# A graph network on one core: ScalarE waits for TensorE's finished products before each half group, and inserts pauses

## The reference, cut to what matters

```python
# layer 0, x is (12500, 128)
msg = relu((x[src] * w[:, None]) @ W_msg + b_msg)
agg = segment_sum(msg, dst, num_segments=12500)
x = layernorm(x + relu(agg @ W_out + b_out))
# layers 1 and 2, with residual and layernorm around both
xt  = einsum('nd,rde->rne', h, W)            # 8 relations
agg = segment_sum(xt[rel, src], dst, num_segments=12500)
h = relu(agg + h @ SW + b)
# out = layernorm(x + h)
```

## Time and profile before

| | us |
|---|---|
| median of 3 runs | 7146.97 (7138.85 to 7151.41) |
| the profiled execution | 7199.0 |
| its span | 7197.2 |
| GpSimdE busy in it | 4549.9 |
| VectorE busy | 2687.2 |
| TensorE matmuls busy | 2514.6 |
| ScalarE busy | 608.2 |

### The profile page before, as it was taken

How to read it: one execution, slowest core, us unless ns; L and a number is a source line. 1 busy time by engine, 2 the same in 40 slices (tenths; PEclk the granted TensorE clock), 3 DMA queues, 4 the chain that set the end, 5 groups by cost and what they waited for, 6 DMA issues and landing times.

```text
span 7197.2 us, 44937 instructions
## 1 busy us (share of the span) xinstructions
PE 2514.6 (35%) x11886; PEld 2050.0 (28%) x11886; DVE 2687.2 (37%) x5889; ACT 608.2 (8%) x1334; POOL 4549.9 (63%) x4832
## 2 busy tenths in 40 slices
PE   4333344333444333433333343333222222222223
PEld 4332233222333322322222233222222222222222
DVE  3777566666555532332222332232111111111112
ACT  2111111111111110000000000000000000000000
POOL 4666666666666646666666666665666666666665
PEclk9666666666666666666666666665556565555556
DMA  5122222222222212222222222221111111121111
GB/s 144 43 79 74 69 73 71 74 70 75 72 72 74 74 58 63 69 69 69 66 70 68 69 69 66 67 68 56 52 51 51 52 51 52 52 53 52 51 51 48
DMA packets 265650, 468.76 MB, mean 65 GB/s; under 512 B 102413, under 2 KB 155317, under 8 KB 265381
## 3 DMA queue, kind: packets, MB, share of 16 engines
q0 software_dynamic: 154016, 315.73, 16.9%
q1 hardware_dynamic: 110212, 149.64, 6.1%
q10 hardware_dynamic: 1152, 0.39, 0.0%
HBM read 343.36 MB, written 122.05 MB: 65 GB/s over the span
## 4 chain that ended last, share of the span: by engine, by line
another core or an unknown queue 48%; DVE 23%; issue 17%; PE 9%; DVEq 2%; ACT 1%; DMA 0%; POOL 0%; SPq 0%; ACTq 0%; POOLq 0%
PE bank L787 5%; DVE rows L763 5%; DVE onehot L745 4%; PE bank L1047 3%; DVE picked L1087 3%; DVE place L1099 2%; DVE tab L1108 1%; DVEq L771 1%; DVE agg L776 1%; DVE bank L1410 1%; DVE work L1411 1%; DVE bank L1408 1%; DVE y L1143 1%; DVE stats L1147 1%
## 5 line engine op out<-in xcount | busy, mean ns | idle before, releaser
L698 POOL DMA_INDIRECT rows<-rel_table,rel_index x3152 | 2973.6, 943 | 1664.4 <-issue 931.5
L787 PE MATMUL bank<-onehot,rows 128*128 128x128 f32 x9626 | 1772.3, 357 | 3320.3 <-issue 1405.4
L787 PEld LDWEIGHTS bank<-onehot,rows 128*128 128x128 f32 x9626 | 1659.1, 265 | 3512.7 <-issue 1537.6
L698 POOL DMA_INDIRECT rows<-msg_table,msg_index x1597 | 1508.8, 945 | 929.0 <-issue 464.7
L776 DVE TENSOR_TENSOR agg<-agg,bank 128x128 f32 x602 | 171.4, 285 | 3613.6 <-remote 3150.7
L745 DVE TENSOR_TENSOR onehot<-bank,place 128x1024 f32<-128x1024 f32 x602 | 728.4, 1210 | 10.6 <-ACT agg L964 3.8
L1047 PE MATMUL bank<-wr,feat 128*128 128x512 f32 x784 | 521.3, 801 | 395.4 <-ACT feat L979 322.0
L763 DVE SCALAR_TENSOR_TENSOR rows<-rows,weight,bank 128x128 f32<-128x128 f32 x1597 | 428.6, 341 | 0.1
L1099 DVE TENSOR_REDUCE place<-picked 128x128 f32<-128x1024 f32 x196 | 367.4, 1875 | 19.8 <-DVE picked L1087 0.5
L668 ACT ACTIVATE rows<-rows 128x512 f32<-128x512 f32 x416 | 260.8, 629 | 1250.7 <-DVE rows L763 705.8
L1047 PEld LDWEIGHTS bank<-wr,feat 128*128 128x128 f32 x784 | 194.2, 275 | 564.8 <-ACT feat L979 332.5
(11 more groups left out here) (123 smaller groups left out, 1285.0 us busy)
## 6 DMA issues: line engine op xcount, KB each, us to landing
rel_table<-tab SPq DMA_DIRECT2D x196, 512.0 KB
rows<-rel_table,rel_index POOLq DMA_INDIRECT x3152
rows<-msg_table,msg_index POOLq DMA_INDIRECT x1597
x_dram<-normed SPq DMA_DIRECT2D x98, 64.0 KB
xin<-x_dram SPq DMA_DIRECT2D x98, 64.0 KB
xin<-in_x_dram SPq DMA_DIRECT2D x97, 64.0 KB
out_dram<-normed SPq DMA_DIRECT2D x97, 64.0 KB
tab<-in_x_dram SPq DMA_DIRECT2D x24, 256.0 KB
```

The lines of the kernel that those rows point to most:

```text
L698: nc.gpsimd.indirect_dma_start(rows[:, u, t, :], None, table, bass.IndirectOffsetOnAxis(ap=table_index[:, g, t:t + 1], axis=0)).then_inc(e ...
L787: ins = nc.tensor.matmul(ps_edge[k][:, 0:P], tile, onehot[:, k, t, :], start=t == 0, stop=t == tiles - 1)
```

## The change

For each half group of each layer, ScalarE now waits until the products that TensorE has been given so far are finished: for the first half, until `prod` tells that the group before is done; for the second half, until a new semaphore `half` tells that the first half's products are done. In layer 0 the wait stands ahead of the ReLU. In layers 1 and 2 it stands ahead of the wait for the rows, and is followed by a pause: a 128 by 512 copy by ScalarE into a scratch tile, and a wait for its end. In layers 0 and 1 the two table products of a block, the self product and the join are also parted: TensorE waits for `go` before the second, the self product and the join, and ScalarE gives `go` after it has seen the piece before finished and has paused. ScalarE's first node step of a block also waits for one more group's products. No product, gather or store is added or removed.

```diff
+        def act_pause():
+            pauses[0] += 1
+            nc.scalar.activation(breath, wr[0][:, 0:512], ACT.Copy).then_inc(s_breath, 1)
+            nc.scalar.wait_ge(s_breath, pauses[0])
+
+        def products_idle(layer, sems, st, h):
+            if st.late or layer not in SPACED:
+                return
+            if h:
+                nc.scalar.wait_ge(sems.half, st.n + 1)
+            else:
+                need(nc.scalar, sems.prod, st.n)
+            if layer:
+                act_pause()
...
                 if layer == 0:
                     nc.scalar.wait_ge(sems.scaled, st.n * 2 + (h + 1))
+                    products_idle(layer, sems, st, h)
...
                 else:
+                    products_idle(layer, sems, st, h)
                     nc.scalar.wait_ge(sems.rows[st.u][h], gathered(st, h))
                     nc.scalar.sem_inc(sems.ready, 1)
...
-            ins.then_inc(sems.prod, 1)
+                ins.then_inc(sems.prod if h else sems.half, 1)
...
                     nc.scalar.wait_ge(edge_main.added, min(groups, COUNT[layer]) + FIRST[layer])
+                    if layer in SPACED:
+                        nc.scalar.wait_ge(edge_main.prod,
+                                          min(groups + 1, COUNT[layer]) + FIRST[layer])
...
+        def act_spacing(layer, sems, stage):
+            st = stage(PRODUCTS[layer]) if layer < 2 else None
+            if st is not None:
+                nc.scalar.wait_ge(sems.part, st.n + 1)
+                act_pause()
+                nc.scalar.sem_inc(sems.go, 1)
+                nc.scalar.wait_ge(sems.prod, st.n + 1)
+                if batch_end(st) and not short_batch(st):
+                    act_pause()
+                    nc.scalar.sem_inc(sems.go, 1)
+                    nc.scalar.wait_ge(sems.own, st.n + 1)
+            st = stage(PRODUCTS[layer] + 2) if layer < 2 else None
+            if st is not None and batch_end(st):
+                act_pause()
+                nc.scalar.sem_inc(sems.go, 1)
...
                 for h in range(2):
+                    if h and spaced:
+                        nc.tensor.wait_ge(sems.go, gone(st.n))
...
+                    if not h:
+                        ins.then_inc(sems.part, 1)
...
+                    if spaced:
+                        nc.tensor.wait_ge(sems.go, gone(st.n) + 1)
                     pe_own(layer, sems, st, trim)
...
+                if layer in SPACED:
+                    nc.tensor.wait_ge(sems.go, gone_join(st.n))
```

More of the change, by code:

```diff
@@ L122, in build @@
     LAGS = (LAG, LAG_TRIM, LAG_TRIM)
+    SPACED = (0, 1, 2)
     RD = R * D
@@ L201, in build @@
         fault = sb("fault", [1, 2])
+        breath = work[:, 7 * GROUP - 512:7 * GROUP]
         base2 = msg_index[0:1, GROUPS:, :].rearrange("p g t -> p (g t)")
@@ L290, in __init__ @@
                     self.joined = sem(f"{name}_joined")
+                    self.go = sem(f"{name}_go")
+                    self.part = sem(f"{name}_part")
                 if table:
@@ L297, in build @@
         s_cut = sem("s_cut")
+        s_breath = sem("s_breath")
         s_pool_turn = sem("s_pool_turn")
@@ L310, in __init__ @@
                 self.prod = sem(f"{name}_prod")
+                self.half = sem(f"{name}_half")
                 self.added = sem(f"{name}_added")
@@ L657, in act_index @@
                     "p g t -> p (g t)"), ACT.Copy).then_inc(sems.index, 1)
+        pauses = [0]
+        def act_pause():
[11 more added lines that the diff above has]
+                act_pause()
         def act_ready(layer, sems, st):
@@ L985, in act_first, with gone, gone_join @@
                                          ).then_inc(sems.sums, 1)
+        def gone(b):
+            return b + 1 + b // UNROLL + max(b - 1, 0) // UNROLL
+        def gone_join(b):
+            return min(b + 2, BLOCKS) + (b + 1) // UNROLL + b // UNROLL + 1
+        def act_spacing(layer, sems, stage):
[13 more added lines that the diff above has]
+                nc.scalar.sem_inc(sems.go, 1)
         def act_nodes(layer, stage, trim):
@@ L1010, in act_nodes @@
                                      ).then_inc(sems.feat, 1)
+            if trim and layer in SPACED:
+                act_spacing(layer, sems, stage)
             if not trim:
@@ L1045, in pe_nodes @@
                 nc.tensor.wait_ge(sems.feat, st.n + 1)
+                spaced = trim and layer in SPACED
                 for h in range(2):
+                    if h and spaced:
+                        nc.tensor.wait_ge(sems.go, gone(st.n))
                     ins = nc.tensor.matmul(table_banks(layer, st, trim)[h][:, :],
```

## The result

The changed kernel takes **7629.6 us** (7601.3 to 7652.6), the kernel before 7147.1: a ratio of **1.0675, 95% interval 1.0637 to 1.0712**, or +482 us where +1053 was forecast. The profiled execution is 7652.6 us with a span of 7650.5, 453 more than the span before. In a second comparison the two stood at 7605.1 and 7147.6, ratio 1.0639 (1.0580 to 1.0698), or +458 us.

A forecast was written before the change was run, and what follows sets the result against it. Gathers set the pace, with GpSimdE's stops from late-told products open to change; +207, +365 and +410 in layers 2, 1 and 0 (+980) on 7199 gave 8180, less 52 is 8130, with two layer starts of 35 each 8200; range 7450 to 9000.

The forecast's parts named there:

- What bounds the kernel: All layers: gathers set the pace; GpSimdE's stops, 771 us in all, come from TensorE's products being told late.
- The first rival: All layers: products lag because TensorE gets work on top of unfinished work; waiting removes 771 us of stops, 6300 to 6500; 16%.
- The price of a record: TensorE beside gathers: each matmul record is told finished at 2.80 us, read at the start of layer 2.
- 21 free: TensorE in a run of gathers: about 21 matmul records are told finished without lag, read at the start of layer 2.
- Stops every 2.2, 1.9 and 1.7 groups: GpSimdE in layers 2, 1 and 0: supply 8 + 21 + T / 2.80 meets demand at T = 22.4, 18.6, 16.9 us.
- A stop of 5.7 and 6.7 us: GpSimdE: 4.2 us lag plus 1.5 for the second half in layer 2; 1.0 more for table products in layers 0 and 1.
- Layer 0, +410: Layer 0: stops cost 3.9 us a group against 1.98 now, +2.0 x 208 groups = +410 us.
- The layer starts, +70: Starts of layers 1 and 2, outside the stretches: they serialise too, an estimated 35 us each.
- Small loss: GpSimdE's stops at the lower bound but as frequent as computed: +0 to +300 us, 7165 to 7450; 8%.
- Nothing moves: Whole kernel: ScalarE's waits are mostly satisfied when it reaches them, or gains and losses meet: 7147 us; 4%.
- shorter stops pay: GpSimdE: a stop after 16 gathers is 1.9 us shorter than after 32 and might shrink to the hop: 7000 us; 6%.
- each group its own stop: GpSimdE: records told freely do not return at short stops, so each group waits, +5.6 x 602: up to 10,500 us; 6%.

The follow-up runs named there:

- the half-group kernels: Two kernels: the changed kernel without parted node work, 7458.0 us (ratio 1.0365); the same also without the pauses in `act_ready`, 7380.7 us (1.0255).
- the direct DMAs: Kernel before, with layer 2's rows brought by SyncE's direct DMAs in table order instead of GpSimdE's indirect ones: 5790.4 against 7184.2 us, ratio 0.8059.
- half the products: Kernel before, with layer 2 multiplying 4 of a group's 8 tiles, gathers unchanged: 7157.9 against 7184.2 us, ratio 0.9959.
- a kernel with nearly the whole change: Changed kernel without ScalarE's wait for one more group's products in `act_first`, run when nothing lagged: 6417.2 against 6087.2 us, ratio 1.0541.

## Why the prediction was right or wrong, point by point

**What bounds the kernel: right.** Gathers stay 1.25 us apart (6013.45 and 6014.70 above), and nearly all that layers 1 and 2 lost is GpSimdE standing. That products are told late, that this goes with GpSimdE gathering, and that one half at a time would make it stand more, held in the changed kernel, in the half-group kernels and, turned round, with the direct DMAs. It held only at times when products lag at all, which the forecast took for granted. The first rival, that the backlog is the cause, is out: a half that waited for the one before is still 10.4 us late. The sign, slower, was right too.

**The price of a record: the step that failed.** "2.80 us for one matmul record" was read off one group at the start of layer 2, told at 4991.59, when GpSimdE had gathered for 81 us without a stop. That group's products had ended 47 us before (the row above of 4942.04), with another group open behind them. The runs of the steady state are 10 to 40 us long. In these a half of the changed kernel costs 0 to 3 us in the first 15 us and 8 to 11 after that, 1.3 a record in the cycle above. The check that the forecast made on it, 67 records told for 66 in a cycle, agreed by its choice of "21 free": two constants from one place, tested at another where they could both be off. With a fixed price, half the products should have moved the kernel by 150 us and more; they moved it 26.

**Stops every 2.2, 1.9 and 1.7 groups.** Counting the gaps over 1.5 us in the timelines of GpSimdE: every 3.4 groups in layer 2 (57 in 193), every 2.1 in layer 1 (92) and every 1.6 in layer 0 (109 in 172). In the trace of before they were 3.7, 2.8 and 2.0. Layer 2 was the miss, and it is where the price went in: 1.3 instead of 2.80 in the forecast's own equation gives 3.3 groups there. It also gives 2.5 and 2.2 in layers 1 and 0, which were nearly right before, so another constant does not save that sum. Nor is the division into stops steady: the second trace of the changed kernel has 72 stops in 194 groups of layer 2, one in 2.7, each 4.4 us long, while the standing in these stops is 1.74 us a group in place of 1.85.

**A stop of 5.7 and 6.7 us: mis-sized in layer 1.** Measured, less the usual 0.3: 6.0 in layer 2, 3.9 in layer 1, 4.5 in layer 0 (before: 5.4, 4.4 and 3.6). The term took 4.2 for the lag and then added the second half, its pause and, for layers 0 and 1, a table product to each stop. In layer 1 the stops have nothing of this: 3.9 is shorter than the row used for the lag alone. That mis-sized term makes most of the +365 that came out as +65: 3.9 / 2.1 = 1.9 us a group against 3.5 forecast.

**Layer 0, +410: the cover that wasn't there; half right in size by chance.** The forecast charged all of it to lag. Where nothing lags a kernel with nearly the whole change still loses 252 us there and none in the other layers. The sentence that failed is "With nothing lagging a group needs 2 x (2.1 + 1.0) = 6.2 us ... covered". It counted ScalarE and TensorE, and tested the cover for layer 1, whose VectorE has 637 us of work in 2140. Layer 0 has 1441 in 2250, 15 us of the 20 that two groups' gathers take, and it is VectorE that waits for what ScalarE has queued behind its new waits. The text named that queue and gave it no price. For the 205 us lost where products lag this is argued, not shown, as no run parts the two there; but VectorE's time adds up in the same way, 15.6 us of work and 9.8 of waits out of 26.1 for two groups, with 4.0 and 4.1 of the waits ahead of the root and the picked columns and 1.5 ahead of the additions, where the kernel before waited 5.1 for those.

**The layer starts, +70.** Measured +87, and +23 at the end, which wasn't in the sum. There every piece is serial, and 62 of the 110 go when the pauses go. The 788 pauses ahead of the halves are covered otherwise: 1.0012 by themselves.

**The sum against the median.** The profile stood 52 us over the runs before and 23 over them after.

**The rivals.** "Small loss" (+0 to +300) had stops at the lower bound, 0.9 us, and they were 3.9 to 6.0; layers 1 and 2 and the starts lost 250 us, inside its range, by chance. Its price didn't follow from its condition either: 0.9 us every 2.2, 1.9 and 1.7 groups is 0.4 to 0.5 us a group, less than the 1.55 to 1.98 of before, and so a gain of some 765 us. "Nothing moves", "shorter stops pay" and "each group its own stop" fell. The forecast's own range, 7450 to 9000, held the time, and so did the wide one.

## What to carry to other kernels

Where completions are told late, a wait for one's own last piece of work can cost that lateness once for each wait in series, so count the completions in series for each block: one wait for a group here cost 0.4%, a second one inside it, with the one ahead of the node work, 2.1% more. Before calling such a chain covered, take the engine that has most work in that stage, here VectorE in layer 0, add up what its stream waits for behind the new waits, and compare with the pace of the stage. A rate must be read in the state in which it will be used: a lateness from an 80 us run of gathers says little about runs of 20. And run the kernel before beside every variant: here it came in two conditions 15% apart, and a comparison across them would have been worth nothing.

## What the runs showed of the hardware

In the traces of 7147 to 7650 us, while GpSimdE starts an indirect DMA every 1.25 us, a finished product of TensorE is told late: by 0 to 2 us after 4 to 7 gathers, by 9 to 13 us after 12 to 15, by 17.8 after 28 to 35 and by 47 in the worst case. The kernel's time and GpSimdE's stops change neither with what the product reads nor with its columns (ratios 1.0007 and 1.0011), and little with how many there are (0.9959). SyncE's direct DMAs at 134 GB/s make nothing late. A float32 matmul of 64 columns took as long as one of 128 here (16 in 3.68 and 3.78 us). GpSimdE in the kernel before stands 1.7 and 1.55 us for each 10 us of gathers in layers 1 and 2, and this sum stayed at 273 to 289 us in layer 2, 1.5 to 1.6 us a group, whether products were halved, read a constant, or GpSimdE rested in small pieces. Why it is this sum is open. And the same program, on the same two chips, at other times had no such lateness at all, beside the same indirect DMAs at the same 1.25 us, and ran 15% faster, 6087 against 7148 us; what switches it was not found. In that condition the kernel before runs at the bare pace of its gathers.
